# A prenorm phase mixer with a ternary FFN on one core: new orders for VectorE and ScalarE

## What is computed

```python
# layer 1, on layernorm(x)
omega = einsum('bsd,ed->bse', x, W_omega) + b_omega
phi = cumsum(omega * exp(log_scale) / sqrt(position), axis=1)
cm_real, cm_imag = x * cos(phi), x * sin(phi)
mem_real = cumsum(cm_real, axis=1) / position
mem_imag = cumsum(cm_imag, axis=1) / position
ret_real = mem_real * cos(phi) + mem_imag * sin(phi)
ret_imag = mem_imag * cos(phi) - mem_real * sin(phi)
h = layernorm(concat(cm_real, cm_imag, ret_real, ret_imag)) * ln_gamma + ln_beta
x = x + (x_normed + gelu(h @ W1.T + b1) @ W2.T + b2)
# layer 2, on layernorm(x), with weights rounded to -1, 0, 1
x = x + relu(layernorm(x) @ Wq1.T + b1) @ Wq2.T + b2
```

## Time and profile before

| | |
|---|---|
| median of 3 runs | 1623.66 us (1623.33 to 1623.72) |
| profiled execution | 1623.21 us, span 1621.1 us |
| TensorE matmul busy | 1530.3 us, 94% |
| VectorE busy | 1470.2 us, 91% |
| ScalarE busy | 1241.1 us, 77% |
| POOL busy | 348.0 us, 21% |
| chain that ended last | VectorE 42%, ScalarE 26%, issue 24%, TensorE 3%, POOL 3% |
| granted TensorE clock | 0.987 of full in the mean, 1.0 from 115 us to 1589 us |

### The profile page before, as it was taken

One profiled execution on the slowest core, in us unless ns is written; L12 is line 12 of the kernel. 1 busy time (PEld: TensorE's weight loads), 2 busy tenths in 40 slices (PEclk: granted clock), 3 DMA queues, 4 the chain that ended last, 5 costly groups with the idle time before them and its releaser, 6 DMA issues.

```text
span 1621.1 us, 31250 instructions
## 1 busy us (share of the span) xinstructions
PE 1530.3 (94%) x11177; PEld 925.6 (57%) x11177; DVE 1470.2 (91%) x2448; ACT 1241.1 (77%) x1773; POOL 348.0 (21%) x235
## 2 busy tenths in 40 slices
PE   3689999999999999999999999999999999999995
PEld 2455556566555665655566565556665555656553
DVE  7999999999999999999999999999999999999843
ACT  6678877787887787787777788777778777877843
POOL 1221222121122212212222211222221222222110
PEclk9899999999999999999999999999999999999998
DMA  5001111100111101111110111111001111010011
GB/s 201 14 14 27 40 40 40 36 16 26 39 39 39 39 24 28 26 39 39 39 39 13 26 39 39 39 39 36 16 26 39 39 39 39 23 28 15 27 27 39
DMA packets 109079, 57.95 MB, mean 36 GB/s; under 512 B 73456, under 2 KB 107504, under 8 KB 109040
## 3 DMA queue, kind: packets, MB, share of 16 engines
q1 hardware_dynamic: 107408, 53.77, 11.7%
q10 hardware_dynamic: 1632, 3.67, 0.6%
HBM read 23.87 MB, written 16.78 MB: 25 GB/s over the span
## 4 chain that ended last, share of the span: by engine, by line
DVE 42%; ACT 26%; issue 24%; PE 3%; POOL 3%; DVEq 1%; ACTq 1%; DMA 0%; SPq 0%; POOLq 0%
ACT arena L624 8%; ACT arena L599 6%; DVE ph L1054 5%; DVE mr L1086 5%; DVE mi L1078 4%; ACT arena L633 4%; DVE arena L1136 4%; DVE ph L1046 3%; DVE bn L1179 2%; DVE cmi L1071 2%; DVE xl L1038 2%; DVE rows L1196 2%; DVE x L1172 2%; DVE cmr L1069 2%; ACT xf L614 2%
## 5 line engine op out<-in xcount | busy, mean ns | idle before, releaser
L817 PE MATMUL ps<-arena,w_hi 128*128 128x512 f16 x2048 | 609.0, 379 | 2.9 <-DVE arena L1136 1.7
L817 PE MATMUL ps<-arena,w_lo 128*128 128x512 f16 x1024 | 388.0, 379 | 0.0
L817 PEld LDWEIGHTS ps<-arena,w_hi 128*128 128x128 f16 x2048 | 197.8, 98 | 223.7 <-issue 2.1
L848 PE MATMUL ps<-fw_t,arena 128*128 128x256 f16 x2048 | 254.6, 272 | 17.0 <-DVE arena L1204 16.0
L832 PE MATMUL ps<-turned,fw_t 128*128 128x512 f16 x1024 | 253.5, 381 | 13.0 <-DMA turned<-rows 13.0
L848 PEld LDWEIGHTS ps<-fw_t,arena 128*128 128x128 f16 x2048 | 191.5, 97 | 92.9 <-issue 58.0
L494 POOL TENSOR_TENSOR sqr<-sqr,turn 128x1024 f32<-128x1024 f32 x32 | 75.4, 2357 | 677.5 <-DVE arena L1136 677.5
L1204 DVE TENSOR_TENSOR arena<-arena 128x512 f16<-128x512 f32 x256 | 172.2, 683 | 41.6 <-ACT arena L633 41.4
L624 ACT ACTIVATE arena<-ps,relu_bias,relu_scale 128x512 f32<-128x512 f32 x256 | 194.1, 770 | 13.4 <-PE ps L832 13.3
L867 PE MATMUL ps<-w_hi,arena 128*128 128x256 f16 x1024 | 183.4, 273 | 0.0
L817 PEld LDWEIGHTS ps<-arena,w_lo 128*128 128x128 f16 x1024 | 100.1, 98 | 120.9
(11 more groups left out here) (190 smaller groups left out, 2739.7 us busy)
## 6 DMA issues: line engine op xcount, KB each, us to landing
x_rows<-in_L_attn_x SPq DMA_DIRECT2D x32, 512.0 KB, 3.5
out<-x SPq DMA_DIRECT2D x32, 512.0 KB, 2.9
arena<-in_L_attn_W ACTq DMA_DIRECT2D x1, 2048.0 KB, 11.2
arena<-in_L_ffn_W SPq DMA_DIRECT2D x2, 1024.0 KB, 10.4
turned<-rows SPq DMA_TRANSPOSE x128, 2.4
arena<-in_L_attn_ln_gamma ACTq DMA_DIRECT2D x1, 512.0 KB, 6.5
pos_rsqrt<-in_positions SPq DMA_DIRECT2D x1, 512.0 KB, 15.1
arena<-in_L_attn_ln_beta ACTq DMA_DIRECT2D x1, 512.0 KB, 12.7
```

The lines of the kernel that those rows point to most:

```text
L817: last = pe.matmul(ps[:, 4 + m], w[:, k, m * P:(m + 1) * P], a[:, c.b, k], start=(i == 0), stop=(i == len(passes) - 1))
L848: last = pe.matmul(ps_rows_a[:, j], a[:, m % SLOTS, j * P:(j + 1) * P], fw2_t[:, m], start=False, stop=(m == KF - 1 and a is rl), skip_gro ...
```

## The change

VectorE and ScalarE get other orders of the same operations, in the loop's step and in the steps outside it. `phase_sums(far)` runs at the end of a step, behind `phase_turns(far)` and the statistics, and not at the beginning of the next. `sin_cos` is split into `sine` and `cosine`, `modulate` into an imaginary and a real half, `gelu` and `first_out` into two each. The imaginary (sine) half goes first everywhere. `context_variance` is moved up ahead of `second_lo` and `sums_real`, `gains_1` behind `memory_imag`. The carry copies are made only for a first half of a sequence; the semaphores that counted them then count by 2. On ScalarE `sums_hi` is the first of the next step, `square_real` the last of its own, and the one-element Sine that loads the table comes at the step's end. `relu_lo` 6 and 7 stand behind the last two `context_lo`.

```diff
 def phase_sums(c):
     need(dve, u_done, c)
-    need(dve, ycarry_done, c, 1)
+    if c.b:
+        need(dve, ycarry_done, c)
...
     last.then_inc(y_done, 1)
-    need(dve, y_done, c)
-    dve.tensor_copy(ph_carry[:, :, :], ph[:, :, CH - 1:CH]).then_inc(ycarry_done, 1)
+    if not c.b:
+        need(dve, y_done, c)
+        dve.tensor_copy(ph_carry[:, :, :], ph[:, :, CH - 1:CH]).then_inc(ycarry_done, 2)
...
 def step(s):   # VectorE
-    if ahead:
-        phase_sums(ahead)
     if now:
         lean_2(now)
...
+    if ahead:
+        modulate_imag(ahead)
+        sums_imag(ahead)
+        modulate_real(ahead)
+        memory_imag(ahead)
     if far:
         gains_1(far)
-    if ahead:
-        modulate(ahead)
-    if now:
-        second_lo(now)
-    if ahead:
-        sums_imag(ahead)
     if nxt:
         context_variance(nxt)
     if far:
         unit_squares(far)
+    if now:
+        second_lo(now)
     if ahead:
         sums_real(ahead)
-        carries(ahead)
-        memory_imag(ahead)
...
     if nxt:
         statistics_2(nxt)
         spread_2(nxt)
+    if far:
+        phase_sums(far)
...
 def step(s):   # ScalarE
+    if nxt:
+        sums_hi(nxt)
     if ahead:
-        act.activation(idle_sine[:, :], half_pi[:, 0:1], ACT.Sin)
         whole_turns(ahead)
+        base_scaled(ahead)
+        sine(ahead)
     if now:
         normalise_2(now)
     if ahead:
-        sin_cos(ahead)
+        cosine(ahead)
...
     if ahead:
+        square_imag(ahead)
         context_hi(ahead, 2, rr_done, rr[:, :, :])
         context_hi(ahead, 3, ri_done, ri[:, :, :])
-        sums_hi(ahead)
+    if now:
+        relu_hi(now, 6)
+        relu_hi(now, 7)
+    if ahead:
+        square_real(ahead)
+    if far:
+        act.activation(idle_sine[:, :], half_pi[:, 0:1], ACT.Sin)
```

More of the change, by code:

```diff
@@ L568, in sin_cos, with cosine @@
                 act.activation(sn[:, :, :], ph[:, :, :], ACT.Sin, scale=-TWO_PI).then_inc(sin_done, 1)
+            def cosine(c):
+                need(act, frac_done, c)
+                act.activation(turn[:, :, :], ph[:, :, :], ACT.Abs).then_inc(abs_done, 1)
                 need(act, abs_done, c)
@@ L661, in step @@
                     gelu(nxt, 1)
+                    gelu_hi(nxt, 0)
+                    gelu(nxt, 2)
+                    gelu_hi(nxt, 1)
+                if now:
+                    relu(now, 0)
                 if nxt:
-                    gelu(nxt, 2)
+                    gelu_hi(nxt, 2)
                 if nxt and not now:
                     gelu(nxt, 3)
+                    gelu_hi(nxt, 3)
                     for n in SIGN_GROUPS:
                         group_hi(n)
-                for m in range(KF):
-                    if now:
-                        relu(now, m)
-                        if m:
-                            relu_hi(now, m - 1)
-                    if m == 3 and nxt and now:
-                        gelu(nxt, 3)
-                    if m == 4 and ahead:
-                        square_real(ahead)
-                    if m == 5 and far:
-                        first_out(far)
-                    if m == 6 and ahead:
-                        square_imag(ahead)
@@ L681, in step @@
-                if now:
-                    relu_hi(now, KF - 1)
+                if now:
+                    relu_hi(now, 0)
+                    relu(now, 1)
+                    relu(now, 2)
+                    relu_hi(now, 1)
+                    relu_hi(now, 2)
+                if nxt and now:
+                    gelu(nxt, 3)
+                if now:
+                    relu(now, 3)
+                    relu_hi(now, 3)
+                if nxt and now:
+                    gelu_hi(nxt, 3)
@@ L683, in step @@
+                if now:
+                    relu(now, 4)
+                    relu(now, 5)
+                    relu_hi(now, 4)
+                if far:
+                    first_turned(far)
+                if now:
+                    relu_hi(now, 5)
+                    relu(now, 6)
+                if far:
+                    first_hi(far)
+                if now:
+                    relu(now, 7)
                 if ahead:
+                    square_imag(ahead)
                     context_hi(ahead, 2, rr_done, rr[:, :, :])
@@ L716, in _ @@
             row_square(1)
-            first_out(first)
+            first_turned(first)
+            first_hi(first)
             row_square(2)
@@ L735, in _ @@
             group_hi(1)
-            sin_cos(first)
+            sine(first)
+            cosine(first)
             normalise_1(second)
@@ L753, in _ @@
             base_scaled(first)
-            sums_hi(first)
+            act.activation(idle_sine[:, :], half_pi[:, 0:1], ACT.Sin)
             prepared(act)
@@ L1392, in _ @@
             unit_squares(second)
-            modulate(first)
+            modulate_imag(first)
+            modulate_real(first)
             sums_imag(first)
             sums_real(first)
-            carries(first)
             dve.wait_ge(p_tab, 16)
@@ L1426, in _ @@
             phase_turns(second)
+            phase_sums(second)
             prepared(dve)
```

108 lines of the change are left out of this document (66 added, 42 removed).

## The result

| | median us | runs | against before |
|---|---|---|---|
| before, same chip | 1623.55 (1623.33 to 1623.72) | 4 | |
| changed | 1635.29 (1634.58 to 1636.47) | 4 | 1.0072, 95% interval 1.0058 to 1.0085 |

What follows compares the result with a forecast made beforehand. VectorE was taken as the bound, nearly matched by TensorE late in the step. Terms -2.4, -1.5, -1.2, +4.2, +4.2 gave +3.3 us a pair, over 14.5 pairs +47 on 1623.2: 1670 us, range 1616 to 1682.

Steps and rivals of the forecast that it cites:

- What bounds: VectorE for two thirds of the step, phase scans to relu 0's remainder; then VectorE and TensorE nearly equal in length.
- `gains_1` behind the memory product, -2.4: Moving lean and gain there on VectorE removes its wait for POOL's inverse standard deviation: 2.4 us saved a pair of steps.
- The sixth remainder's wait, -1.5: Moving relu 6's and 7's remainders behind the last context remainder removes VectorE's wait for ScalarE: 1.5 us saved a pair.
- Carries and cosine, 0: On VectorE, fewer carry copies in odd steps offset new waits and a later cosine: 0 a pair, between -0.4 and +0.6.
- rival A: ScalarE's squares end late, POOL waits out remainder 7, VectorE waits 1.2 for `omega`: +0.3 a pair, 1627 us, chance 0.22.
- Phase scans, 0: Moving VectorE's phase scans to the end of the step before frees ScalarE but changes VectorE's time by 0.
- `qa` against the scans, +4.2 and -1.2: POOL's product holds one `sums_real` scan per step, +4.2 us a pair; its old meeting with the memory product goes, -1.2.
- The sum of squares against remainder 7, +4.2: POOL's L494, waiting before VectorE issues relu 7's remainder, goes first and holds it: +4.2 us a pair.

## Why the prediction was right and wrong, point by point

- **What bounds.** Right: VectorE up to remainder 0, and from there the two engines nearly equal. In the versions without the scan meeting TensorE's length was 46.43 a step; the prediction's 92.9 a pair is twice that.
- **`gains_1` behind the memory product, -2.4.** The wait went, but the term was not this move's: alone it cost 6.4 us, because the cosine's wait stood behind POOL's. The sine-first order belongs to the term.
- **The sixth remainder's wait, -1.5.** It went, through ScalarE's order; putting the remainders back changed nothing.
- **Carries and cosine, 0.** In the even step the cosine is free, in the odd one it waits 0.15. An order with more dependent neighbours pays at its seams: the scan starts at 895.31 behind a product that ends at 895.27, where independent ones overlap by 0.08. By the table of the result all this came to +0.41 a pair, inside the bounds of -0.4 and +0.6: the copies' own records are 0.44 shorter, the gaps at such seams 0.85 longer. With 0.2 more of wait for `omega` it makes up the 0.6 over rival A's price; no run tests the seams by themselves.
- **Phase scans, 0.** Right, shown by moving them back.
- **`qa` against the scans, +4.2 and -1.2.** Right in place and in size: one scan of 3.37 in every step. Undoing it gave back 2.2 to 2.5 a pair, since the memory product pays again and TensorE catches up. `qa` was issued 1.23 us behind `cve`, where the text had 1.35 to 1.45, and so 0.34 ahead of the scan.
- **The sum of squares against remainder 7, +4.2.** This step failed. The schedule under it was right: it had ScalarE's square done 21.4 us behind the first scaling and remainder 7 issued at 21.8, and the trace has 21.3 and 21.7. The price was near: a held remainder takes 2.16 longer, where the text had 2.1, and one hold a step costs about 1.7, where the sum has 1.5 (2.1 less rival A's wait of 0.6). What failed is "POOL would be waiting ... so remainder 7 stands". POOL had waited 0.30 us when remainder 7 started, and was passed over, in all 28 steps in which they met. Its certainty came from meetings with leads of about one microsecond, applied to a lead of a third of that; 0.30 us lay outside what any row of before showed, and the case for rival A was worded as "the squares come too late for the collision" when being there in time was not enough either. Without this term the sum is -0.9, rival A's wait of 0.6 a step brings it to +0.3, and the 0.2 and 0.4 above make it +0.9. That the time still fell near rival A's 1627 is no merit of A's condition: the squares were in time.
- **The arithmetic.** The terms as written give 3.3 x 14.5 = 48, not 47, and the upper bounds 1685 and not 1682; neither bears on the outcome.

The Trainium skill ("SBUF — State Buffer", section "SBUF: two separate sides") says that the first of the two keeps the port pair for its whole instruction and the other fully blocks. These runs agree on that: a scan of 3.37, a remainder of 2.84, L494 at 3.20 when it is the one to wait. The same section says under "Who interferes with whom" that issue order decides who blocks. By POOL's issue as the trace has it that foretells `qa`, but not remainder 7, before which POOL was issued 0.30 us and did not run; when VectorE's next operation counts as issued, no record here shows. There the forecast rested on a guess.

## What to carry to other kernels

When a POOL operation of 2 us with SBUF operands becomes ready under a run of VectorE operations with two SBUF inputs, price a hold of its full length beside the case of none, and move its input so that it becomes ready where VectorE reads PSUM: here one moved line was worth 38 us. When a wait is removed, look at what the same engine waits for next and whether it was hidden under the first; `gains_1` alone made the kernel slower. A time that hangs on two engines being 0.3 us apart is two forecasts, and both want a real chance.

## What the runs showed that was not expected

POOL being ready is not enough to get in between two VectorE operations: it was passed over at leads of 0.30 and 0.36 us, behind an extra subtraction even at 0.96, and let in at 0.29, 0.34, 0.35 and 0.39 elsewhere. A second, short POOL operation behind a long one gets in as well when VectorE was held by the first (L496, 1.60, then a remainder of 1.75). And a perfect separation over hundreds of steps (the table load) did not survive one run that moved the load.
